# A state-space layer and a gated FFN: the norm's shift on ScalarE, twelve products with C on GpSimd, a new order of jobs

## The chip, the cores and the metric

One core of a Trainium2 chip runs one program. The metric is the device time of one execution in microseconds (us). TensorE multiplies and transposes, VectorE and ScalarE work on 128 partitions side by side, GpSimd (POOL in the profile) does elementwise products too, and SyncE (SP) issues the DMAs.

## What is computed

For 16 sequences of 1024 tokens with 256 channels: a selective scan with 16 states per channel, a residual and a layer norm, then a gated FFN with quantized weights, a residual and a second norm. The reference, cut:

```python
xz = jnp.einsum('btd,pd->btp', x, W_xproj)         # 64 for dt, 16 B, 16 C
dt = jax.nn.softplus(jnp.einsum('btr,dr->btd', dt_raw, W_dt) + b_dt)
dA = jnp.exp(dt[..., None] * A)
dBx = dt[..., None] * Bm[:, :, None, :] * x[..., None]
def step(h, inp):
    h = dA_t * h + dBx_t
    y = jnp.einsum('bds,bs->bd', h, C_t)
out = ys + Dp * x
x = _layernorm(x + out)
h = jax.nn.silu(gate) * up                          # 256 -> 768 -> 256
x = _layernorm(x + jnp.einsum('bsh,dh->bsd', h, wd))
```

A layer norm is (x - mean) * rstd, written in the kernel as x * rstd + shift with shift = -mean * rstd.

## The kernel before

Tokens come in 32 chunks of 512, two per sequence. An even chunk starts its scans from zero (`par` 0), the odd one from the last column of the even one's, which ScalarE keeps in `h_carry` (`carry`, L490). The Python loops write out all 32 chunks for each engine.

A chunk is 16 units, one for each state s. Channels lie on the partitions in two halves (q = 0, 1). For a state: ScalarE makes the decay exp(dt * a) (`decay`, L504); dt * x * B comes from GpSimd (`times_b`, L398, read from `b_bc`, rows of B that a DMA spreads over the partitions) or, for the six `K_STATES`, from ScalarE in token layout (`times_b`, L518) and TensorE, which transposes it into `p_da` (`ub_transposed`, L896). VectorE scans each half (L699, 1024 in all). The product with C is GpSimd's for the states of `POOL_STATES` (`times_c`, L408) and VectorE's for the other five (L707), with C spread by TensorE transposes into `p_c` (L905). TensorE sums all states in `p_y` (L922).

`p_da` has one PSUM bank for each half. A decay of a state that is not in `K_STATES` goes there too, and waits until the scan before has read the bank. Decays of `K_STATES` go to `da_k` in SBUF, `DA_LEAD` units ahead.

The other jobs belong to the chunk before (norm 1, gate, up, hidden), to the one two before (down, norm 2, store) or to the next one (transpose, projection, softplus, dt, u). `AT` gives each a unit and a zone in it (up to 5 zones, in each engine's own order); an engine's queue is in that order, and nothing overtakes. Their sequence: x is transposed, copied (`x_out`), projected; `rank_out` and `bc_out` copy out; `project_dt`, three activations and `dt_of` (VectorE, L675) give dt; `u_of` is GpSimd's (L387). Norm 1: `z_out`, statistics (L713) and means (L717) on VectorE, log and exp on ScalarE (L547, L552), `shifts` on VectorE for both norms in one operation of 8 columns, four normalizations (L529), transposes (`x1_transposed`), `x1_high` (ScalarE, L534), `x1_low` (VectorE, L727), six gate products (L953), each with a silu (L538) behind a table load, a table load back (`exp_table`, L542), six up products (L964) and six hidden products (L733). Gate and up share the two banks of `p_m`, so gate j waits for silu j-2. Then down (L977), `residual` (L740) and norm 2 (L559).

SyncE issues the spread of B in runs of states (L335) and of C by state (L342), each as soon as its buffer is free. A store waits in the same queue at unit `STORE_AT`. The shift, as it stands (L722):

```python
def shifts(call, k=slice(0, 2)):
    dve.wait_ge(s_rstd, call)
    nc.vector.scalar_tensor_tensor(shift[:, k, :], mean_var[:, k, :, 0], -1.0, rstd[:, k, :],
                                   ALU.mult, ALU.mult).then_inc(s_ln, 1)
```

## Time and profile before

| | |
|---|---|
| median of 3 runs | 1906.5 us (1903.86 to 1908.56) |
| profiled execution | 1904.62 us, span 1902.8 us |
| busy: PE, DVE, ACT, POOL | 1703.2 (90%), 1754.1 (92%), 1599.5 (84%), 1639.2 (86%) us |
| first scan to the end of the last | 27.0 to 1854.5 us |
| granted TensorE clock | 0.984 of full speed |

The names PE, DVE, ACT and POOL stand for TensorE, VectorE, ScalarE and GpSimd. In a row of a timeline the columns are the start in us, the time taken, engine, line, operation, what it writes and reads, how many are merged, and in brackets how long the engine stood idle before it and who ended that. In a row of a group the numbers behind the bars are busy us and mean ns of one, and the engine's idle us before them. Neighbours on one engine overlap by 0.05 to 0.1 us in the records, so the distance of two starts is the cost of the first.

### The profile page before, as it was taken

How to read it: one execution, taken by the hardware profiler on the slowest of the kernel's cores; microseconds unless marked ns; L12 is line 12 of the kernel's file. 1: busy time of each engine (PE TensorE's matmuls, PEld its weight loads, DVE VectorE, ACT ScalarE, POOL GpSimd, SP SyncE). 2: the span in 40 equal slices, each digit the busy share in tenths (PEclk: the TensorE clock that was granted, in tenths of full speed). 3: DMA queues.
4: the chain of work that ended last, by engine and by line, in shares of the span. 5: the costliest groups of instructions: out<-in, count | busy, mean ns of one | idle time of the engine just before them, and what ended most of it. 6: DMA issues, size and time to landing. Idle time of an engine off the chain costs nothing. (4 is left out here: it accounts for less than half of the span.)

```text
span 1902.8 us, 33164 instructions
## 1 busy us (share of the span) xinstructions
PE 1703.2 (90%) x11048; PEld 1339.9 (70%) x11048; DVE 1754.1 (92%) x2060; ACT 1599.5 (84%) x2992; POOL 1639.2 (86%) x710
## 2 busy tenths in 40 slices
PE   5789999998999999999998999989999999999977
PEld 3566777776777776777776777766777777777765
DVE  4999999999999999999999999999999999999993
...
GB/s 240 128 93 76 141 135 136 83 108 100 141 135 129 96 100 103 140 135 137 83 113 96 141 135 130 96 99 102 141 135 135 81 110 101 141 135 118 73 12 23
DMA packets 107419, 216.51 MB, mean 114 GB/s; under 512 B 10129, under 2 KB 44530, under 8 KB 107250
## 3 DMA queue, kind: packets, MB, share of 16 engines
...
q14 instruction: 79, 0.65, 0.1%
HBM read 195.48 MB, written 18.87 MB: 113 GB/s over the span
## 5 line engine op out<-in xcount | busy, mean ns | idle before, releaser
L408 POOL TENSOR_TENSOR h<-h,c_bc 128x1024 f32<-128x1024 f32 x352 | 830.3, 2368 | 122.3 <-ACT h_carry L490 62.3
L398 POOL TENSOR_TENSOR ub<-u,b_bc 128x1024 f32<-128x1024 f32 x320 | 753.3, 2368 | 0.1
L504 ACT ACTIVATE p_da<-dt,neg_a 128x512 f32<-128x512 f32 x640 | 435.1, 683 | 126.9 <-DVE h L699 121.2
L922 PE MATMUL p_y<-ident,h 128*128 128x128 f32 x4096 | 530.4, 278 | 5.2 <-POOL h L408 3.8
L922 PEld LDWEIGHTS p_y<-ident,h 128*128 128x128 f32 x4096 | 478.5, 144 | 37.6 <-issue 19.8
L699 DVE TENSOR_TENSOR_SCAN h<-p_da,h_carry,ub 128x512 f32<-128x512 f32 x320 | 392.6, 1264 | 6.6 <-ACT p_da L504 4.3
L699 DVE TENSOR_TENSOR_SCAN h<-p_da,ub 128x512 f32<-128x512 f32 x320 | 375.7, 1206 | 20.3 <-ACT p_da L504 13.0
L977 PE MATMUL p_o<-wt_down,hid 128*128 128x256 f32 x1536 | 347.3, 379 | 2.4 <-DVE res L740 1.6
L518 ACT ACTIVATE ub_t<-u_t,bc_t 128x256 f32<-128x256 f32 x768 | 341.6, 496 | 0.0
L977 PEld LDWEIGHTS p_o<-wt_down,hid 128*128 128x128 f32 x1536 | 286.8, 190 | 53.1 <-issue 14.7
L896 PE MATMUL p_da<-ident,ub_t 128*128 128x128 f32 x1536 | 236.2, 278 | 79.3 <-ACT ub_t L518 49.0
L504 ACT ACTIVATE da_k<-dt,neg_a 128x512 f32<-128x512 f32 x384 | 269.9, 711 | 0.0
L896 PEld LDWEIGHTS p_da<-ident,ub_t 128*128 128x128 f32 x1536 | 174.6, 142 | 129.7 <-ACT ub_t L518 81.2
L699 DVE TENSOR_TENSOR_SCAN h<-da_k,h_carry,p_da 128x512 f32<-128x512 f32 x192 | 237.2, 1263 | 2.7 <-PE p_da L896 2.1
L699 DVE TENSOR_TENSOR_SCAN h<-da_k,p_da 128x512 f32<-128x512 f32 x192 | 225.9, 1204 | 0.8 <-issue 0.3
L707 DVE TENSOR_TENSOR h<-h,p_c 128x1024 f32<-128x1024 f32 x160 | 190.8, 1192 | 0.7 <-ACT h_carry L490 0.6
L733 DVE SCALAR_TENSOR_TENSOR hid<-p_m,hid 128x512 f32<-128x512 f32 x188 | 125.2, 680 | 62.1 <-PE p_m L964 61.8
L964 PE MATMUL p_m<-x_t,wt_up 128*128 128x512 f16 x744 | 180.8, 379 | 0.1
L953 PE MATMUL p_m<-x_t,wt_gate 128*128 128x512 f16 x744 | 173.1, 378 | 0.3 <-ACT hid L538 0.3
L905 PE MATMUL p_c<-ident,bc_t 128*128 128x128 f32 x640 | 99.3, 279 | 72.2 <-DVE h L707 72.2
L387 POOL TENSOR_TENSOR u<-dt,x_t 128x1024 f32<-128x1024 f32 x32 | 75.7, 2365 | 91.2 <-DVE dt L675 91.2
L538 ACT ACTIVATE hid<-p_m 128x512 f32<-128x512 f32 x190 | 110.0, 597 | 49.4 <-PE p_m L953 48.9
...
## 6 DMA issues: line engine op xcount, KB each, us to landing
c_bc<-bc_rows_dram SPq DMA_DIRECT2D x352, 256.0 KB, 6.3
...
```

The source lines that it names most:

```text
L398: nc.gpsimd.tensor_tensor(ub[:, i % UB_SLOTS, :, :], u[:, par, :, :], b_bc[:, i:i + 1, :].broadcast_to([P, DH, T]), ALU.mult).then_inc(s_u ...
L408: nc.gpsimd.tensor_tensor(h[:, s % H_SLOTS, :, :], h[:, s % H_SLOTS, :, :], c_bc[:, i:i + 1, :].broadcast_to([P, DH, T]), ALU.mult).then_i ...
L504: nc.scalar.activation(da, dt[:, par, q, :], ACT.Exp, scale=neg_a[:, q, s:s + 1]).then_inc(done, 1)
L518: nc.scalar.activation(ub_t[:, i % K_SLOTS, k, :], u_t[:, k, :], ACT.Identity, scale=bc_t[:, par, k, s:s + 1]).then_inc(s_ubt, 1)
L699: nc.vector.tensor_tensor_scan(h[:, s % H_SLOTS, q, :], da, dbx, initial, ALU.mult, ALU.add).then_inc(s_scan, 1)
L707: nc.vector.tensor_tensor(h[:, s % H_SLOTS, :, :], h[:, s % H_SLOTS, :, :], p_c[:, :, :].broadcast_to([P, DH, T]), ALU.mult).then_inc(s_hc ...
L733: nc.vector.scalar_tensor_tensor(hid[:, j, :], p_m[:, j % 2, :] if bank is None else bank, 1.0 / (QUANT * X1_SCALE), hid[:, j, :], ALU.mul ...
L896: ins = nc.tensor.transpose(p_da[:, q, k * P:(k + 1) * P], ub_t[:, i % K_SLOTS, k, q * P:(q + 1) * P], ident[:, :])
L922: ins = nc.tensor.matmul(p_y_tok[:, k, q * P:(q + 1) * P], h[:, s % H_SLOTS, q, k * P:(k + 1) * P], ident[:, :], start=(s == SUM_ORDER[0] ...
L953: ins = nc.tensor.matmul(p_m[:, j % 2, :], wt_gate[:, n % DH, j * P:(j + 1) * P], x1_t[:, n // DH, n % DH, :], start=(n == 0), stop=(n == ...
L964: ins = nc.tensor.matmul(p_m[:, j % 2, :], wt_up[:, n % DH, j * P:(j + 1) * P], x1_t[:, n // DH, n % DH, :], start=(n == 0), stop=(n == 2 ...
L977: ins = nc.tensor.matmul(p_o[:, k % 2, :], hid[:, j, k * P:(k + 1) * P], wt_down[:, j, :], start=(j == 0), stop=(j == NH - 1))
```

## The change

- `shifts` is now 8 ScalarE activations of one column, -mean * rstd with the scale read from `rstd`. VectorE makes the negated means ahead of it (`negate`, one operation on 8 columns of one tensor).
- State 5's product with C goes from VectorE to GpSimd.
- `K_STATES` has 7 and 13 for 9 and 14. Slots are counted on over the chunks.
- `first_wait` issues a wait only where its engine has not yet waited for that value. In places waits change their order.
- `carry` is one unit later on ScalarE, behind the jobs of zone 0.
- Most entries of `AT` move.
- At the start VectorE makes `u` and the first product with B. At the end the last chunk's hidden values get a buffer of their own, the silus go ahead of norm 2 of the chunk before, TensorE's order is changed, and norm 2 and the store go in two halves.

The diff, cut (the many `first_wait` lines are of the form shown):

```diff
-POOL_STATES = (0, 1, 2, 3, 4, 7, 9, 10, 11, 13, 14)
+POOL_STATES = (0, 1, 2, 3, 4, 5, 7, 9, 10, 11, 13, 14)
 
 
 UB_AHEAD = 3
 
 C_LAG = 1
+CARRY_LAG = 1
+CARRY_ZONE = 0
...
-    "weights": (7, 1), "x_transposed": (0, 4), "x_out": (0, 2), "project": (2, 1), "rank_out": (4, 0),
-    "bc_out": (3, 1), "project_dt": (3, 3), "softplus_abs": (5, 1), "softplus_exp": (5, 1),
-    "softplus_log": (5, 3), "dt_of": (7, 0), "u_of": (7, 0), "u_transposed0": (12, 2), "u_out0": (14, 0),
-    "u_transposed1": (14, 3), "u_out1": (14, 2), "z_out": (2, 0), "stats1": (4, 0), "mean1": (5, 1),
-    "norm_log": (6, 0), "norm_exp": (6, 0), "shifts": (6, 1), "norm1_0": (6, 2), "norm1_1": (7, 1),
-    "norm1_2": (7, 1), "norm1_3": (7, 1), "x1_transposed": (8, 0), "x1_high": (8, 0), "x1_low": (8, 2),
-    "gate0": (9, 3), "gate1": (9, 3), "gate2": (10, 1), "gate3": (10, 2), "gate4": (10, 2), "gate5": (10, 2),
-    "silu0": (9, 1), "silu1": (9, 1), "silu2": (9, 2), "silu3": (10, 0), "silu4": (10, 0), "silu5": (10, 0),
-    "exp_table": (10, 0), "up0": (10, 2), "up1": (10, 2), "up2": (13, 0), "up3": (13, 1), "up4": (13, 4),
-    "up5": (14, 3), "hidden0": (11, 0), "hidden1": (11, 0), "hidden2": (13, 1), "hidden3": (14, 0),
-    "hidden4": (15, 0), "hidden5": (15, 0), "skip0": (8, 2), "skip1": (6, 1), "down0": (0, 3), "down1": (1, 0),
-    "down2": (1, 0), "down3": (1, 2), "down4": (2, 4), "down5": (2, 4), "down6": (3, 0), "down7": (3, 2),
-    "residual0": (1, 2), "residual1": (4, 2), "stats2": (5, 1), "mean2": (5, 2), "norm2_0": (11, 1),
-    "norm2_1": (11, 2), "norm2_2": (14, 3), "norm2_3": (15, 1), "bc_turned": (6, 0), "bc_cols": (9, 2),
+    "weights": (7, 1), "x_transposed": (0, 4), "x_out": (1, 3), "project": (2, 3), "rank_out": (3, 3),
+    "bc_out": (3, 0), "project_dt": (4, 0), "softplus_abs": (5, 1), "softplus_exp": (5, 1),
+    "softplus_log": (6, 1), "dt_of": (7, 2), "u_of": (8, 0), "u_transposed0": (12, 3), "u_out0": (14, 1),
+    "u_transposed1": (14, 3), "u_out1": (14, 1), "z_out": (2, 1), "stats1": (4, 1), "mean1": (5, 1),
+    "norm_log": (5, 2), "norm_exp": (6, 0), "negate": (6, 1), "shifts": (6, 1), "norm1_0": (7, 1),
+    "norm1_1": (7, 1), "norm1_2": (7, 1), "norm1_3": (7, 3), "x1_transposed": (8, 0), "x1_high": (8, 1),
+    "x1_low": (8, 2), "gate0": (9, 3), "gate1": (9, 3), "gate2": (10, 1), "gate3": (10, 1), "gate4": (10, 2),
+    "gate5": (10, 2), "silu0": (9, 0), "silu1": (9, 0), "silu2": (9, 1), "silu3": (9, 3), "silu4": (10, 0),
+    "silu5": (10, 1), "exp_table": (10, 1), "up0": (10, 2), "up1": (10, 2), "up2": (11, 1), "up3": (11, 3),
+    "up4": (13, 1), "up5": (13, 4), "hidden0": (11, 0), "hidden1": (11, 0), "hidden2": (12, 0),
+    "hidden3": (12, 2), "hidden4": (14, 2), "hidden5": (14, 2), "skip0": (8, 2), "skip1": (7, 2),
+    "down0": (0, 2), "down1": (0, 4), "down2": (1, 1), "down3": (1, 1), "down4": (3, 1), "down5": (3, 1),
+    "down6": (3, 2), "down7": (3, 2), "residual0": (2, 0), "residual1": (5, 0), "stats2": (5, 1),
+    "mean2": (5, 2), "norm2_0": (12, 0), "norm2_1": (12, 2), "norm2_2": (13, 0), "norm2_3": (14, 3),
+    "bc_turned": (5, 4), "bc_cols": (10, 3),
 }
...
-K_STATES = (2, 6, 9, 10, 14, 15)
+K_STATES = (2, 6, 7, 10, 13, 15)
 K_AHEAD = 2
 K_SLOTS = 2
-LATE = 13
-STORE_AT = 11
-DA_LEAD = {6: 2, 9: 3, 10: 2, 14: 2}
+LATE = 12
+STORE_AT = 7
+DA_LEAD = {6: 2, 7: 3, 10: 2}
...
-            if not isinstance(value, int) or value > 0:
+            if value > 0:
                 eng.wait_ge(s, value)
+
+        waited = {}
+
+        def first_wait(eng, s, value):
+
+            first = value > waited.get((eng, s.name), 0)
+            if first:
+                waited[eng, s.name] = value
+            return first
...
+        def slot_freed(eng, states, c, i, slots):
+
+            n = len(states) * c + i - slots
+            if n >= 0:
+                value = DH * units(n // len(states), states[n % len(states)])
+                if first_wait(eng, s_scan, value):
+                    eng.wait_ge(s_scan, value)
...
-                store(c)
+                for a in range(2):
+                    sp.wait_ge(s_out_ready, TT * (c + 1) + 2 * (a + 1))
+                    sp.dma_start(out_chunks[c][:, 2 * a:2 * a + 2, :],
+                                 res_n[:, 2 * a:2 * a + 2, :]).then_inc(s_out, 16)
             over_chunks(sp, step, tail)
-            sp.wait_ge(s_out, 16 * (CHUNKS + 1))
+            sp.wait_ge(s_out, 16 * (CHUNKS + 2))
...
             def times_c(c, s, par, batch):
                 i = POOL_STATES.index(s)
-                pool.wait_ge(s_c[i], 16 * (c + 1))
-                wait(pool, s_scan, 2 * units(c, s))
                 if par == 0:
                     pool.wait_ge(s_carry, units(batch, s))
+                elif first_wait(pool, s_scan, 2 * units(c, s)):
+                    pool.wait_ge(s_scan, 2 * units(c, s))
+                pool.wait_ge(s_c[i], 16 * (c + 1))
                 nc.gpsimd.tensor_tensor(h[:, s % H_SLOTS, :, :], h[:, s % H_SLOTS, :, :],
                                         c_bc[:, i:i + 1, :].broadcast_to([P, DH, T]),
                                         ALU.mult).then_inc(s_hc_pool, 1)
 
-            u_of(0, 0)
-            for s in range(UB_AHEAD):
+            for s in range(1, UB_AHEAD):
...
+            def shifts(call, norms=range(2), tiles=range(TT)):
+                act.wait_ge(s_rstd, call)
+                act.wait_ge(s_neg, call)
+                for n in norms:
+                    for t in tiles:
+                        ins = nc.scalar.activation(shift[:, n, t:t + 1], neg_mean[:, n, t:t + 1], ACT.Identity,
+                                                   scale=rstd[:, n, t:t + 1])
+                ins.then_inc(s_ln, 1)
+
+            def norm2(c, call, k, halves=2):
+                if first_wait(act, s_ln, call):
+                    act.wait_ge(s_ln, call)
+                if first_wait(act, s_res, 2 * c + halves):
+                    act.wait_ge(s_res, 2 * c + halves)
...
-                        if core and par == 0 and zone == 3:
-                            carry(c, s)
+                        if zone == CARRY_ZONE:
+                            cq, sq, pq = unit_at(c, s, -CARRY_LAG, par)
+                            if pq == 0 and (core if s >= CARRY_LAG else prev):
+                                carry(cq, sq)
 
             def tail(c):
                 z_out(c)
                 norm_log(c + 1, c + 1, 0, slice(0, 1))
                 norm_exp(c + 1, slice(0, 1))
+                shifts(c + 1, range(1))
                 for k in range(TT):
                     norm1(c, k, x_in)
                 x1_high(c)
+                for j in range(NH):
+                    silu(c, j, tail_ps[j % 4], tail_hid)
+                exp_table()
                 norm_log(c + 2, 0, c, slice(1, 2))
                 norm_exp(c + 2, slice(1, 2))
-                for j in range(NH):
-                    silu(c, j, tail_ps[j % 4])
+                shifts(c + 2, range(1, 2))
                 for k in range(TT):
                     norm2(c - 1, c + 2, k)
-                exp_table()
-                norm_log(c + 3, 0, c + 1, slice(1, 2))
-                norm_exp(c + 3, slice(1, 2))
-                for k in range(TT):
-                    norm2(c, c + 3, k)
+                for a in range(2):
+                    act.wait_ge(s_mean[1], c + 1 + a)
+                    half = slice(2 * a, 2 * a + 2)
+                    nc.scalar.activation(log_var[:, 1, half], mean_var[:, 1, half, 1], ACT.Ln,
+                                         bias=eps[:, :]).then_inc(s_log_var, 1)
+                    act.wait_ge(s_log_var, c + 3 + a)
+                    nc.scalar.activation(rstd[:, 1, half], log_var[:, 1, half], ACT.Exp,
+                                         scale=-0.5).then_inc(s_rstd, 1)
+                    shifts(c + 3 + a, range(1, 2), range(2 * a, 2 * a + 2))
+                    for k in range(2 * a, 2 * a + 2):
+                        norm2(c, c + 3 + a, k, a + 1)
...
                 i = DVE_STATES.index(s)
                 dve.wait_ge(s_c_ps, ND * c + (i + 1))
-                wait(dve, s_scan, 2 * units(c, s))
                 if par == 0:
                     dve.wait_ge(s_carry, units(batch, s))
+                elif first_wait(dve, s_scan, 2 * units(c, s)):
+                    dve.wait_ge(s_scan, 2 * units(c, s))
                 nc.vector.tensor_tensor(h[:, s % H_SLOTS, :, :], h[:, s % H_SLOTS, :, :],
                                         p_c[:, :, :].broadcast_to([P, DH, T]),
                                         ALU.mult).then_inc(s_hc_dve, 1)
...
-            def shifts(call, k=slice(0, 2)):
-                dve.wait_ge(s_rstd, call)
-                nc.vector.scalar_tensor_tensor(shift[:, k, :], mean_var[:, k, :, 0], -1.0, rstd[:, k, :],
-                                               ALU.mult, ALU.mult).then_inc(s_ln, 1)
+            def negate(call, c1, c2, k=slice(0, 2)):
+                wait(dve, s_mean[0], c1)
+                wait(dve, s_mean[1], c2)
+                wait(dve, s_ln, call - 1)
+                nc.vector.tensor_scalar_mul(neg_mean[:, k, :], mean_var[:, k, :, 0], -1.0).then_inc(s_neg, 1)
...
+            dve.wait_ge(s_dt, 1)
+            dve.wait_ge(s_xt, 1)
+            nc.vector.tensor_tensor(u[:, 0, :, :], dt[:, 0, :, :], x_t[:, 0, :, :], ALU.mult).then_inc(s_u, 1)
+            dve.wait_ge(s_u, 1)
+            dve.wait_ge(s_b[0], 16)
+            nc.vector.tensor_tensor(ub[:, 0, :, :], u[:, 0, :, :], b_bc[:, 0:1, :].broadcast_to([P, DH, T]),
+                                    ALU.mult).then_inc(s_ub_first, 1)
...
                 norm_mean(0)
+                negate(c + 1, c + 1, 0, slice(0, 1))
                 residual(c - 1, 0)
-                shifts(c + 1, slice(0, 1))
                 x1_low(c)
                 residual(c - 1, 1)
-                dve.wait_ge(s_res, 2 * c)
+                if first_wait(dve, s_res, 2 * c):
+                    dve.wait_ge(s_res, 2 * c)
                 norm_stats(1, res)
                 dve.wait_ge(s_stats[1], TT * c)
                 norm_mean(1)
-                shifts(c + 2, slice(1, 2))
+                negate(c + 2, 0, c, slice(1, 2))
                 for j in range(NH):
-                    hidden(c, j, tail_ps[(NH + j) % 4])
+                    hidden(c, j, tail_ps[(NH + j) % 4], tail_hid)
                 for a in range(2):
+                    half = range(2 * a, 2 * a + 2)
                     residual(c, a, x_in)
-                dve.wait_ge(s_res, 2 * (c + 1))
-                norm_stats(1, res)
-                dve.wait_ge(s_stats[1], TT * (c + 1))
-                norm_mean(1)
-                shifts(c + 3, slice(1, 2))
+                    dve.wait_ge(s_res, 2 * c + a + 1)
+                    norm_stats(1, res, half)
+                    dve.wait_ge(s_stats[1], TT * c + 2 * (a + 1))
+                    norm_mean(1, half)
+                    dve.wait_ge(s_mean[1], c + 1 + a)
+                    nc.vector.tensor_scalar_mul(neg_mean[:, 1, 2 * a:2 * a + 2], mean_var[:, 1, 2 * a:2 * a + 2, 0],
+                                                -1.0).then_inc(s_neg, 1)
...
-                for i in range(6):
+                for i in range(4):
                     down(c - 1, i // 2, i % 2, CHUNKS)
                 x1_transposed(c, False, True, x_in)
+                for i in range(4, 6):
+                    down(c - 1, i // 2, i % 2, CHUNKS)
+                for j in range(4):
+                    tail_gate(c, j)
                 for i in range(6, 8):
                     down(c - 1, i // 2, i % 2, CHUNKS)
-                for j in range(NH):
+                for j in range(4, NH):
                     tail_gate(c, j)
                 for j in range(NH):
                     tail_up(c, j)
                 for i in range(8):
-                    down(c, i // 2, i % 2, CHUNKS)
+                    down(c, i // 2, i % 2, CHUNKS, tail_hid)
```

## Rows read from the trace of the kernel before

**Rows 1.** busy time by stretch: an odd chunk, an even chunk.

```profile
993.30:1051.60 58.30, 52.35 (x347) 41.02 (x346) 55.99 (x65) 49.08 (x86) 51.93 (x23) 1.00 0.35 117
1051.60:1107.30 55.70, 51.48 (x344) 40.77 (x343) 52.77 (x65) 50.33 (x100) 50.41 (x23) 1.00 0.37 117
```

**Rows 2.** timeline of VectorE in the even chunk from 1051.63.

```profile
1051.63 2.31 DVE L699 TENSOR_TENSOR_SCAN h<-p_da,ub 128x512 f32<-128x512 f32 x2
...
1090.38 0.69 DVE L733 SCALAR_TENSOR_TENSOR hid<-p_m,hid 128x512 f32<-128x512 f32 x1 [1.85 <-PE p_m L964]
...
1092.15 5.88 DVE L699 TENSOR_TENSOR_SCAN h<-p_da,ub 128x512 f32<-128x512 f32 x5 [0.22 <-ACT p_da L504]
```

**Rows 3.** timeline of ScalarE in the same even chunk.

```profile
1063.68 0.58 ACT L461 COPY rank_t<-p_m 64x512 f32<-64x512 f32 x1
1064.17 0.91 ACT L518 ACTIVATE ub_t<-u_t,bc_t 128x256 f32<-128x256 f32 x2
...
1083.72 1.28 ACT L538 ACT_TABLE_LOAD   x1
```

**Rows 4.** timeline of ScalarE and VectorE in the odd chunk from 993.26.

```profile
1006.07 0.91 ACT L518 ACTIVATE ub_t<-u_t,bc_t 128x256 f32<-128x256 f32 x2
...
1027.05 1.28 ACT L538 ACT_TABLE_LOAD   x1
...
1036.11 5.98 DVE L699 TENSOR_TENSOR_SCAN h<-p_da,h_carry,ub 128x512 f32<-128x512 f32 x5 [0.22 <-ACT p_da L504]
```

**Rows 5.** waits of ScalarE from 1006.0 to 1027.1.

```profile
ACT p_da L504 <- DVE h L699: 1.3, 3, 0.7
ACT x L529 <- DVE shift L722: 0.6, 1, 0.6
```

**Rows 6.** timelines: the shift in four chunks, one GpSimd product.

```profile
98.25 5.08 DVE L722 SCALAR_TENSOR_TENSOR shift<-mean_var,rstd 128x8 f32<-128x8 f32 x1
100.92 2.38 POOL L408 TENSOR_TENSOR h<-h,c_bc 128x1024 f32<-128x1024 f32 x1
...
1014.30 2.08 DVE L722 SCALAR_TENSOR_TENSOR shift<-mean_var,rstd 128x8 f32<-128x8 f32 x1
...
1072.37 0.47 DVE L722 SCALAR_TENSOR_TENSOR shift<-mean_var,rstd 128x8 f32<-128x8 f32 x1 [0.30 <-ACT rstd L552]
...
1813.33 4.67 DVE L722 SCALAR_TENSOR_TENSOR shift<-mean_var,rstd 128x8 f32<-128x8 f32 x1
```

**Rows 7.** groups of instructions over the whole span.

```profile
L490 ACT COPY h_carry<-h 128x2 f32<-128x2 f32 x256 | 46.1, 180 | 0.7 <-DVE h L699 0.3
L717 DVE BATCH_NORM_AGGREGATE mean_var<-stats 128x2 f32<-128x6 f32 x256 | 23.0, 152 | 0.1
L547 ACT ACTIVATE log_var<-mean_var,eps 128x8 f32<-128x8 f32 (+1 forms) x34 | 9.9, 292 | 25.0 <-DVE mean_var L717 25.0
L552 ACT ACTIVATE rstd<-log_var 128x8 f32<-128x8 f32 (+1 forms) x34 | 7.1, 208 | 1.1
L1043 PE MATMUL p_m<-x_t,wt_gate 128*128 128x512 f16 x16 | 3.8, 378 | 1.8 <-ACT hid L538 1.8
```

**Rows 8.** the page, its parts 5 and 6.

```profile
L408 POOL TENSOR_TENSOR h<-h,c_bc 128x1024 f32<-128x1024 f32 x352 | 830.3, 2368 | 122.3 <-ACT h_carry L490 62.3
...
c_bc<-bc_rows_dram SPq DMA_DIRECT2D x352, 256.0 KB, 6.3
```

**Rows 9.** timeline of VectorE at the start: the first scan.

```profile
26.96 1.22 DVE L699 TENSOR_TENSOR_SCAN h<-p_da,ub 128x512 f32<-128x512 f32 x1 [4.96 <-POOL ub L398]
```

**Rows 10.** the chain that ended last, its end (start us, us, what).

```profile
1894.80 1.42 DVE stats L713 x4
...
1898.51 0.98 ACT res_n L559 x2
```

**Rows 11.** one line's instructions: the casts (ns min/median/max).

```profile
L671 DVE CAST hid<-hid x2: 952/956/959, 13.5 to 14.4; 128x1536 f32<-128x1536 int32 x2
L671 DVE CAST res<-res x1: 555/555/555, 15.2 to 15.2; 128x768 f32<-128x768 int32 x1
```

190 lines of the change are left out of this document (113 added, 77 removed).

## The prediction

> **What bounds the kernel now.** I read the busy time of each engine in two neighbouring chunks first. The time is made of 32 chunks of 512 tokens, and each chunk is 16 units, one for each state. Chunks come in pairs: an even one of 55.7 us and an odd one of 58.4 us, whose scans start from a carried state. VectorE is busy 52.8 us of the one and 56.0 of the other, GpSimd 50.4 and 51.9, TensorE 51.5 and 52.4, ScalarE 50.3 and 49.1 [rows 1]. So VectorE leads, but four engines lie within some 6 us, and an engine's total does not say which wait ends last. For that I follow one chunk along VectorE and ScalarE.
>
> In the even chunk from 1051.63 VectorE stands still in one place only: for `hidden0`, 1.85 us [rows 2]. Everything ahead of that wait is a chain. ScalarE has no idle time put down to any other engine between its first product with B of state 6, at 1064.17 (12.54 us into the chunk), and the table load ahead of the first silu, at 1083.72 (32.09) [rows 3]. The silus then pace the gate products, and a second table load and a decay stand between the last silu and the scan of state 11, at 1092.15 (40.52). From the first table load to that scan it is 8.43 us, of work that the change leaves as it is. After it VectorE works nearly without idle time for 15.2 us to the chunk's end. So **an even chunk is VectorE's for units 11 to 3, and ScalarE's for units 4 to 10.**
>
> In the odd chunk the same stretch on ScalarE goes from 1006.07 (12.8 us into the chunk) to 1027.05 (33.8), with 1.9 us of waiting for VectorE in it, 0.6 of that for the shift [rows 4, 5]. The scan of state 11 is at 1036.11, 42.85 into the chunk [rows 4]. This stretch was set by VectorE.
>
> **The shift.** It works on 8 elements, and takes 2.08 us in the odd chunk, 0.47 in the even one, 5.08 in chunk 1 and 4.67 in the last [rows 6]. In chunk 1 the last of GpSimd's products ended at 103.30, the shift at 103.33. So it waits for GpSimd, and there for more than two products in a row, each of 2.4 us. Both its inputs lie in SBUF.
>
> **The change, part by part.**
>
> Shift to ScalarE: VectorE loses 2.55 us a pair and gets a negation of 8 elements; one SBUF input, as in the aggregations of 0.15 us [rows 7]. I take 0.1, and the other case is a rival. ScalarE gets 8 activations of one column, each with a scale read from memory. No row has one. The nearest: the exp of 8 columns with a fixed scale lasts 208 ns, the log with a bias from memory 292, the carry's copy 180 [rows 7]. Back to back an operation overlaps the next by 0.09 us (the copy at 1063.68 lasts 0.58, the next starts 0.49 later [rows 3]). So one costs between 0.09 (a copy's spacing) and 0.2 us (292 less the overlap). I take 0.19, since the scale's read is like the log's bias: 1.5 us, with the wait of the first normalization for the last of them 1.6. They stand in unit 6, inside ScalarE's stretch, ahead of four normalizations, so in an even chunk all of it is on the path. The Trainium skill ("ScalarE: Activation LUTs", What ACT_TABLE_LOAD costs) gives 186 ns for an activation, 93 more for each pointer operand and an overlap of 93, which is an estimate of 0.19 too.
>
> `rank_out` from unit 4 to unit 3: it leaves the head of ScalarE's stretch, 0.49 us (1063.68 to 1064.17) [rows 3]. Other jobs of the stretch change places, not number: states 6, 7 and 10 take the way over TensorE where it was 6, 9 and 10, still three products and six pairs of decays. The silus begin in unit 9, as before behind the decays of state 10.
>
> Twelve products on GpSimd: VectorE loses one product, 1.11 us in spacing, in unit 6; GpSimd gets one of 2.37, spacing 2.32. GpSimd then has 23 operations, 53.4 us a chunk [rows 8]. TensorE loses four transposes, 0.6 us. VectorE's saving lies in the stretch that ScalarE sets: nothing in an even chunk, all of it in an odd one up to the point where ScalarE sets that too.
>
> Repeated waits dropped: two scans, each behind two to four waits, take 2.31 us together and leave no gap [rows 2], so I take nothing; bounds 0 and 0.3 us a chunk less.
>
> Jobs moved: `dt_of` goes behind the scans of unit 7. Walking the new order with the spacings of the rows, the x1 transposes start when `norm1_3` ends (27.0), `x1_high` at 28.5 and `x1_low` at 29.6, still ahead of the table load; I find no new wait there over 0.4 us. The two later hidden products come two units earlier, in time for their up products. The carries come one step later on ScalarE. In even chunks that of state 8 falls behind two silus, near 35.5, so VectorE's product of state 8 waits 2 us from 33.4; VectorE would stand before `hidden0`, near 40, anyway, so that is taken from idle time and costs 0 (2 if that wait were gone). GpSimd's products of states 9 and 10 wait for theirs too, in GpSimd's slack. On SyncE's queue the store goes ahead of the transfers of units 7 to 10. These are then issued near the end of a chunk, and are used from unit 5 of the next one, over 15 us later against landings of 6.3 us [rows 8]: nothing.
>
> **The sum for a middle chunk.** Even: ScalarE's stretch starts at 12.0, not 12.54, and its 19.55 us become 21.05 (1.6 more, 0.1 less as a carry moves behind the silus), so the table load is at 33.0, where it was 32.09: 0.9 us longer, 56.6. Odd: start 12.3, work 19.1 plus 1.6, no wait left, table load at 33.0 for 33.8; and the third gate product need not wait for a transpose of state 10 (0.65 us). Together 1.45 us shorter, 56.9. In both the scan of state 11 is then near 41.4. **The gain of the odd chunks is half eaten by the even ones:** 15 times +0.9 and 14 times -1.45 is -6.8; with 0.1 a chunk for small waits, about -9 us over chunks 2 to 30.
>
> **Ends.** Chunk 1: its shift of 5.08 goes, and other waits will take up a part, so -3 (bounds -1, -5). Last chunk: ScalarE has little to do there, and the 4.67 of the shift, the 1.11 of a product and a wait for `x1_high` go, -6 (bounds -3, -8). Start: `u` and the first product with B on GpSimd, for which the first scan waits 4.96 us [rows 9], become two VectorE operations of 1.2; ScalarE's transposed work and the second scan gain only 1.2 of the 2.4. With the product less in chunk 0: -2 (bounds -1, -4). Tail: x1 no longer waits behind the residual for its shift; the gate products lose the 1.8 us in which TensorE stood until the first silu [rows 7]; the last statistics go in halves, so of 4.7 us behind the last residual (1894.80 to 1899.49) 3.1 are left [rows 10]. Downs of the last chunk end 2.4 us earlier: -4 in all (bounds -2.5, -6).
>
> Sum: -9 - 3 - 6 - 2 - 4 = **-24 us**. The profiled execution took 1904.6 us (span 1902.8), which gives 1880.6; it stands 1.9 under the median of the three runs, so **1882**.
>
> **Rivals.**
> 1. *ScalarE's additions are cheap or its stretch has slack.* At 0.09 us each the shifts cost 0.7, the middle chunks gain 0.8 more each: 1882 - 24 = 1858. If VectorE sets the path throughout, the pair loses its 2.5 + 2.2 us in full (less 0.2), 4.5 for my 0.6: some 58 less, 1824 [rows 6, 7]. For: VectorE has the most busy time in rows 1. Against: rows 3.
> 2. *GpSimd becomes the bound.* 53.4 us of work in a chunk of 56.7 leaves 3.3 of idle time, and it waits 5.3 and more in a chunk now (rows 1: 55.7 less 50.4), for `dt_of` and for carries. If these waits stay, a chunk is some 57.4 on average over both kinds, 0.7 more: 1904. For: both waits are in the new order too. Against: with waits at fixed places a later GpSimd waits less.
> 3. *The negation meets the same lock as the shift.* The casts of the weights take 956 ns for 1536 columns and 555 for 768, 0.52 ns a column, half of what a scan or product needs: some one-input operations of VectorE in SBUF work at twice the rate [rows 11]. If the negation does, it waits in unit 6 until GpSimd's run of products (now three: state 4's with C, state 9's with B, state 5's with C) ends, as in chunk 1: from 20.4 to 25.4 into the chunk. VectorE then reaches `dt_of` 5 us late, `x1_high` comes at 31.3 for 28.5, the table load near 35.8 for 33.0. 2.8 us a chunk, 29 times, and 3 and 5 us in chunk 1 and the last: 1882 + 89 = **1971, slower**. It decides from about 2 us of waiting, which is the slack of `x1_low`. Against it: the aggregations, with one input in SBUF too and beside running products, are at 0.15 us in the mean of 256 [rows 7]. The Trainium skill ("SBUF — State Buffer", Who interferes with whom) says just this: tensor_scalar can run in a two-port mode and then shares an exclusive lock with GpSimd. By that rule the change would not do what it says. The trace shows the lock for two inputs and the double rate for a cast, neither for this form.
>
> **Chances.** Forecast 0.54; rival 1 0.18; rival 2 0.12; rival 3 0.16. The range 1842 to 1912 holds the forecast with the bounds of its terms, the cheap half of rival 1 and rival 2, and leaves out rival 3 and VectorE as bound. A measurement here tells 0.3% (6 us) from nothing. Faster 0.71, same 0.13 (rival 2 and the worst of the forecast's ends), slower 0.16.
>
> **What would show it.** The negation at 0.1 to 0.2 us, or at 2 to 5 ending with a GpSimd product. In the chunk's windows, even and odd both near 56.7. The idle time of VectorE before `hidden0` growing from 1.85 to some 3 us, and ScalarE without idle time in units 4 to 8. The shift activations spaced at 0.19 us. GpSimd's idle time shrinking to 3 us a chunk. The forecast fails if the scan of state 11 is not near 41.4 us into its chunk, by a ScalarE that is faster through unit 6 than its rows say, or by one that waits.

## The result: slower, by the rival that had 0.16

| | before | after |
|---|---|---|
| median of 20 runs, us | 1904.1 (1902.4 to 1908.6) | 1934.1 (1908.4 to 1939.8) |
| ratio, with its 95% interval | | 1.0134 [1.0115, 1.0154] |
| profiled execution, us (span) | 1904.6 (1902.8) | 1930.0 (1928.2) |
| granted clock, mean | 0.984 | 0.968 |

The time is outside my range of 1842 to 1912, and on the other side of "no change": slower by 1.3%, clear of the noise. The ratio leaves out the five runs after that are over 1.5% above the fastest of that kernel, so it is below the 1.016 of the two medians. The changed kernel also varies five times as much from run to run as the one before (31 us against 6).

Two rows of the groups of instructions by line (busy us, mean ns of one, idle time before), the first of after, the second of before, name the cause:

```profile
L795 DVE TENSOR_SCALAR neg_mean<-mean_var 128x8 f32<-128x8 f32 (+1 forms) x33 | 92.4, 2799 | 0.1
```

```profile
L722 DVE SCALAR_TENSOR_TENSOR shift<-mean_var,rstd 128x8 f32<-128x8 f32 (+1 forms) x34 | 46.5, 1369 | 5.7 <-ACT rstd L552 5.7
```

I had taken the negation of 8 elements at 0.1 us. Its mean is 2.8 us, twice that of the shift that it replaces. One odd chunk of after, as a timeline of all engines (start, us, engine, line, and in brackets the idle time ahead of it and what ended it), where [rows 6] has the shift at 2.08:

```profile
1142.69 2.36 POOL L442 TENSOR_TENSOR h<-h,c_bc 128x1024 f32<-128x1024 f32 x1
...
1143.79 5.88 DVE L795 TENSOR_SCALAR neg_mean<-mean_var 128x8 f32<-128x8 f32 x1
...
1145.01 2.34 POOL L431 TENSOR_TENSOR ub<-u,b_bc 128x1024 f32<-128x1024 f32 x1
...
1147.31 2.33 POOL L442 TENSOR_TENSOR h<-h,c_bc 128x1024 f32<-128x1024 f32 x1
1149.59 3.76 DVE L769 TENSOR_TENSOR_SCAN h<-da_k,h_carry,p_da 128x512 f32<-128x512 f32 x3
1149.77 1.59 ACT L602 ACTIVATE shift<-neg_mean,rstd 128x1 f32<-128x1 f32 x8 [4.61 <-DVE neg_mean L795]
...
1150.91 1.12 PE L987 MATMUL p_da<-ident,ub_t 128*128 128x128 f32 x4 [6.09 <-DVE h L769]
...
1154.54 2.37 POOL L421 TENSOR_TENSOR u<-dt,x_t 128x1024 f32<-128x1024 f32 x1 [4.89 <-DVE dt L742]
```

The negation starts 1.1 us into one GpSimd product, and lasts past the ends of two, until the third ends at 1149.64 and GpSimd has no next one. ScalarE meanwhile waits 4.61 us for it with the shifts, TensorE 6.09 for a scan behind it, and later GpSimd 4.89 for `dt_of`, which is late too: **all four engines stand, one after the other, for one operation of 8 elements.** The same row in chunk 1, in an even chunk and in the last:

```profile
98.12 7.46 DVE L795 TENSOR_SCALAR neg_mean<-mean_var 128x8 f32<-128x8 f32 x1
...
1087.82 0.51 DVE L795 TENSOR_SCALAR neg_mean<-mean_var 128x8 f32<-128x8 f32 x1
...
1840.81 8.40 DVE L795 TENSOR_SCALAR neg_mean<-mean_var 128x8 f32<-128x8 f32 x1
```

In all 15 even chunks from chunk 2 on it is 0.5 us, and in the 14 odd ones 5.9 us eleven times and 1.3 us three times; each time it ends within 0.1 us of the end of a product. Behind the last product, in the tail, the same form takes 0.17 us (this line: ns min/median/max, first and last start):

```profile
L896 DVE TENSOR_SCALAR neg_mean<-mean_var x2: 169/169/169, 1917.2 to 1923.4; 128x2 f32<-128x2 f32 x2
```

The busy times of the two kinds of chunk, in the columns of [rows 1] (us, then PE, PEld, DVE, ACT, POOL, then the granted clock):

```profile
1067.40:1122.80 55.40, 51.34 (x341) 40.30 (x339) 51.80 (x64) 50.96 (x108) 51.27 (x23) 1.00 0.40 123
1122.80:1183.80 61.00, 53.30 (x344) 41.89 (x343) 58.68 (x64) 49.99 (x94) 55.81 (x25) 0.94 0.38 117
```

VectorE's "busy" time in the odd chunk includes the wait, so 58.7 looks like work. In the even chunk, where the negation waits only 0.5 us, the new order takes 55.4 us for the 55.7 of [rows 1]. The clock in the odd one is 0.94 on average; in the 7 us from 1147.0, which begin inside the 6 us in which TensorE stands idle, it is 0.52, mostly the lower level of 1.2 GHz:

```profile
1147.00:1154.00 7.00, 3.09 (x16) 3.09 (x17) 6.96 (x5) 4.20 (x14) 2.65 (x2) 0.52 0.05 16
```

For all that follows I take the span apart at the first scan of each chunk (us; "even" and "odd" are means over chunks 2 to 30; every row comes from one profiled execution):

| kernel | first scan | chunk 0 | chunk 1 | even (15) | odd (14) | last | tail |
|---|---|---|---|---|---|---|---|
| before | 26.96 | 50.17 | 61.56 | 55.77 | 58.39 | 61.93 | 48.30 |
| after | 24.70 | 53.05 | 63.45 | 55.61 | 60.34 | 63.45 | 44.64 |
| e1, reduction | 24.59 | 55.65 | 56.08 | 55.84 | 55.66 | 54.59 | 44.65 |
| e3, GpSimd waits | 24.88 | 53.21 | 57.56 | 55.74 | 56.17 | 57.08 | 44.65 |
| e4, shifts doubled | 24.94 | 55.77 | 57.55 | 57.94 | 57.51 | 55.97 | 47.41 |
| e6, shift alone, reduction | 25.06 | 50.07 | 59.52 | 57.41 | 58.17 | 57.54 | 52.04 |
| e7, shift alone, multiplication | 25.59 | 50.22 | 62.75 | 57.87 | 59.97 | 62.05 | 50.37 |
| e8, e1 with 11 products | 22.88 | 55.18 | 56.09 | 55.43 | 56.14 | 55.30 | 44.65 |
| e9, shift on GpSimd | 24.76 | 55.75 | 55.43 | 54.27 | 55.01 | 54.29 | 44.65 |
| e10, after with 11 products | 24.80 | 56.08 | 60.86 | 55.43 | 60.18 | 63.65 | 44.65 |

### The profile page after: what moved, and what is told of

It is laid out like the page before. It is cut to its first block and busy times, and to the rows that moved or that the text cites. A ratio compares the mean times of both kernels' runs of the same rounds, so it can differ in the third digit from the quotient of the medians.

```text
span 1928.2 us, 30962 instructions
## 1 busy us (share of the span) xinstructions
PE 1704.6 (88%) x10920; PEld 1340.0 (69%) x10920; DVE 1768.7 (92%) x2031; ACT 1627.2 (84%) x3254; POOL 1710.9 (89%) x740
## 5 line engine op out<-in xcount | busy, mean ns | idle before, releaser
L442 POOL TENSOR_TENSOR h<-h,c_bc 128x1024 f32<-128x1024 f32 x384 | 905.1, 2365 | 86.8 <-ACT h_carry L528 59.8
L987 PE MATMUL p_da<-ident,ub_t 128*128 128x128 f32 x1536 | 243.6, 285 | 135.6 <-DVE h L769 123.5
L1076 PE MATMUL p_o<-wt_down,hid 128*128 128x256 f32 x1488 | 342.8, 380 | 0.0
L1076 PEld LDWEIGHTS p_o<-wt_down,hid 128*128 128x128 f32 x1488 | 275.5, 190 | 48.9 <-issue 14.7
L778 DVE TENSOR_TENSOR h<-h,p_c 128x1024 f32<-128x1024 f32 x128 | 153.8, 1202 | 30.7 <-ACT h_carry L528 30.6
L1051 PEld LDWEIGHTS p_m<-x_t,wt_gate 128*128 128x128 f16 x744 | 64.9, 98 | 100.6 <-ACT hid L581 38.9
L421 POOL TENSOR_TENSOR u<-dt,x_t 128x1024 f32<-128x1024 f32 x31 | 73.4, 2369 | 61.9 <-DVE dt L742 61.5
```

The lines of the kernel that those rows point to most:

```text
L442: nc.gpsimd.tensor_tensor(h[:, s % H_SLOTS, :, :], h[:, s % H_SLOTS, :, :], c_bc[:, i:i + 1, :].broadcast_to([P, DH, T]), ALU.mult).then_i ...
L778: nc.vector.tensor_tensor(h[:, s % H_SLOTS, :, :], h[:, s % H_SLOTS, :, :], p_c[:, :, :].broadcast_to([P, DH, T]), ALU.mult).then_inc(s_hc ...
L987: ins = nc.tensor.transpose(p_da[:, q, k * P:(k + 1) * P], ub_t[:, k_slot(c, i), k, q * P:(q + 1) * P], ident[:, :])
L1051: ins = nc.tensor.matmul(p_m[:, j % 2, :], wt_gate[:, n % DH, j * P:(j + 1) * P], x1_t[:, n // DH, n % DH, :], start=(n == 0), stop=(n == ...
L1076: ins = nc.tensor.matmul(p_o[:, k % 2, :], hid[:, j, k * P:(k + 1) * P], wt_down[:, j, :], start=(j == 0), stop=(j == NH - 1))
```

## Experiments

**e1: the same negation in another form** (here and, in the same way, in the tail). The theory: a multiplication by a constant needs the port to SBUF that GpSimd's products use, and waits until their run is broken. A reduction over one element gives the same 8 numbers without it.

```diff
-nc.vector.tensor_scalar_mul(neg_mean[:, k, :], mean_var[:, k, :, 0], -1.0)
+nc.vector.tensor_reduce(neg_mean[:, k, :], mean_var[:, k, :, 0:1], AxisListType.X, ALU.add, negate=True)
```

> The changed kernel, in which only the form of the negation differs: the mean is negated by a reduction over a dimension of one element (with its result negated) and not by a multiplication with a constant; the same 8 elements, the same place, the same engine, SBUF to SBUF. Theory A (the negation waits for GpSimd's run of products at their common port to SBUF, and the reduction doesn't use that port): the negation takes 0.1 to 0.2 us everywhere, all odd chunks are the 56.2 us that the three undisturbed ones of the changed kernel have, chunk 1 and the last lose 7 us each: 1928 - 11 x 5.3 - 14 - 2 = 1854, between 1848 and 1866. Rival B (8 elements are late for another reason: VectorE waits ahead of it for data, or the new order of the token jobs is itself slower): the long operation stays whatever its form, 1920 to 1940. Rival C (any operation of VectorE between SBUF and SBUF waits for GpSimd): as B. My recorded forecast for the case of a negation that costs nothing was 1882.

Measured: 1853.7 us, 0.9727 [0.9713, 0.9742] of before. The instructions of the negation, by line (ns min/median/max, first and last start):

```profile
L795 DVE TENSOR_REDUCE neg_mean<-mean_var x33: 133/135/157, 99.3 to 1829.0; 128x8 f32<-128x8 f32 x31, 128x4 f32<-128x4 f32 x2
```

One operation's form is the whole loss: 80 us between the medians of two kernels that differ in nothing else. In this form the negation never takes over 157 ns, beside the same products of GpSimd, so rivals B and C fall. The Trainium skill ("SBUF — State Buffer", Who interferes with whom) states that `tensor_scalar` can enter two-port modes and so contend for a pair of ports shared with GpSimd, and that `tensor_reduce` never does on this chip. Both halves agree with the rows: 5.88 us and 0.135.

**e3: GpSimd waits for the multiplication.** The form stays; only GpSimd's run is broken ahead of its product in unit 6.

```diff
+if s == 6 and (prev or last):
+    pool.wait_ge(s_neg, c)
 if core and (sa >= UB_AHEAD or nxt) and sa in B_STATES:
     times_b(ca, sa, pa)
```

> The changed kernel, the negation a multiplication as before, but GpSimd waits for the negation ahead of its product with B in unit 6. So the negation meets one running product at most. Theory A: it ends at the end of that product, 0.5 us in even chunks and 1.3 us in odd ones, GpSimd loses under 0.3 us a chunk; odd chunks near 56.2 and no other change: 1852 to 1868, within 0.4% of the kernel with the reduction. If the order or ScalarE's shifts were the cause instead, odd chunks stay near 61 and the time at 1920 to 1940.

Measured: 1861.0 us, 0.9766 [0.9751, 0.9780]. Timelines of GpSimd and VectorE in an odd chunk:

```profile
1106.41 2.35 POOL L442 TENSOR_TENSOR h<-h,c_bc 128x1024 f32<-128x1024 f32 x1
1108.88 2.35 POOL L431 TENSOR_TENSOR ub<-u,b_bc 128x1024 f32<-128x1024 f32 x1
...
1107.50 1.30 DVE L797 TENSOR_SCALAR neg_mean<-mean_var 128x8 f32<-128x8 f32 x1
```

As expected: the negation ends with the product, at 1108.80, and GpSimd goes on at 1108.88. It is 1.3 us in all 14 odd chunks. Adding a wait to GpSimd took 73 us off the kernel. In chunk 1 the negation comes earlier, passes one end of a product and stops where the added wait stands, at 4.16 us.

**e2: are the dropped waits to blame?** In the helper `first_wait`:

```diff
-return first
+return value > 0
```

> The changed kernel with every repeated wait put back (each engine waits again for what it has already waited for, the negation stays a multiplication). Theory A1 (a run of GpSimd products shuts the negation out whatever stands between them): as the changed kernel, 1920 to 1940, negation near 5.9 us in most odd chunks. Rival A2 (only products without a wait between them follow each other so closely that the negation doesn't get in; the dropped waits are what turned the short wait into a long one): the negation gets in at the next end of a product, 1.3 us in odd chunks, which are then near 56.2: 1860 to 1875.

Measured: 1940.0, 1.0188 [1.0153, 1.0223]. A1 holds: the long negations are there with all waits in place (5.9 us in 11 of the 14 odd chunks, 1.3 in three, and 8.8 in chunk 1).

**e5: and what are the waits worth?** The same edit on e1.

> The kernel with the reduction in place of the multiplication (1853.7), and every repeated wait put back. It prices the dropped waits. My prediction took them at nothing, with bounds 0 and 0.3 us a chunk: 1854 to 1863. The changed kernel with its multiplication gave 1934 and with the waits put back 1940, so the rival, 0.2 us a chunk, gives 1860, and the even and odd chunks of the trace are then each 0.2 longer than 55.8 and 55.7.

Measured: 1855.6, 0.9746 [0.9733, 0.9760], whose interval overlaps that of e1. By the trace a chunk is 0.1 (even, 55.92 for 55.84) and 0.2 us (odd, 55.89 for 55.66) longer, 4 us over the middle chunks, inside my bounds of 0 to 0.3 a chunk. The medians differ by only 2: in the traces, the stretch up to the end of chunk 0 is 3 us shorter with the waits, for no known reason. The 6 us between after and e2 say nothing here: the runs of the one scatter over 31 us and those of the other over 17.

**e4: are ScalarE's shifts on the path?** The 8 activations of e1, done twice.

```diff
+for n in norms:
+    for t in tiles:
+        nc.scalar.activation(shift_2[:, n, t:t + 1], neg_mean[:, n, t:t + 1], ACT.Identity, scale=rstd[:, n, t:t + 1])
 for n in norms:
     for t in tiles:
         ins = nc.scalar.activation(shift[:, n, t:t + 1], ...)
```

> The kernel with the reduction, in which ScalarE computes all 8 shifts twice (8 more activations of one column a chunk, into a tile that nobody reads). It prices the shifts on the path. By the steps of my prediction (units 4 to 10 are set by ScalarE in even and odd chunks, 0.19 us for one) each chunk grows by 1.5 us: 45 us over the kernel with the reduction, some 1900. If VectorE sets these units now, or ScalarE has slack there, it grows by less than 10 us in all. In between, the part of each kind of chunk can be read from its length.

Measured: 1918.4, 1.0065 [1.0048, 1.0081], 64.7 over e1. The timeline of ScalarE in one chunk:

```profile
1084.07 1.57 ACT L603 ACTIVATE shift<-neg_mean,rstd 128x1 f32<-128x1 f32 x8
1085.55 1.57 ACT L607 ACTIVATE shift<-neg_mean,rstd 128x1 f32<-128x1 f32 x8
```

Eight take 1.48 us from start to start, 0.185 each: my 0.19 holds. But a pair of chunks grew by 3.95 us, not 2.96. The rest comes with the clock: the two chunks around these rows have 0.97 each,

```profile
1061.60:1119.10 57.50, 52.48 (x341) 41.88 (x340) 51.59 (x64) 52.51 (x116) 51.28 (x23) 0.97 0.38 117
1119.10:1177.00 57.90, 53.28 (x344) 42.34 (x343) 53.23 (x64) 51.44 (x102) 55.82 (x25) 0.97 0.40 123
```

and in e1 there are even chunks of both kinds, from first scan to first scan 55.43 us at 1.00 and 56.11 at 0.97:

```profile
1028.40:1083.90 55.50, 51.29 (x342) 40.39 (x340) 51.54 (x65) 50.94 (x108) 51.45 (x23) 1.00 0.39 123
...
1139.50:1195.60 56.10, 52.53 (x341) 42.04 (x339) 51.46 (x64) 51.06 (x108) 51.39 (x23) 0.97 0.38 122
```

The two have the same instructions, so a fall of the clock costs 0.7 us there. Compared at an equal clock, the doubled shifts cost just their own length in both kinds: an even chunk at 0.97 takes 57.57 us for 56.11 in e1, an odd one at 1.00 takes 57.14 for 55.66. So all of the 1.48 is on the path. With doubled shifts TensorE waits for the normalized tile 96.7 us in all, with e1 50.6, and 21 of the 29 middle chunks have a clock below 1.00 instead of 9. A term that makes TensorE stand can thus cost more than its own length. It need not: in the kernel before, odd chunks at 0.97 and at 1.00 both take 58.4 us.

**e6 and e7: the shift's change alone.** The kernel before, with nothing changed but the shift: in e6 the negation is the reduction, in e7 the multiplication.

```diff
-dve.wait_ge(s_rstd, call)
-nc.vector.scalar_tensor_tensor(shift[:, k, :], mean_var[:, k, :, 0], -1.0, rstd[:, k, :], ALU.mult, ALU.mult)
...
+wait(dve, s_ln, call - 1)
+nc.vector.tensor_reduce(neg_mean[:, k, :], mean_var[:, k, :, 0:1], AxisListType.X, ALU.add, negate=True)
```

> The kernel before with the norm shift alone changed: VectorE negates the means by the reduction that doesn't wait for GpSimd, at the place of the old shift, and ScalarE computes the shift in 8 activations of one column. By the steps of my prediction: an even chunk gets ScalarE's 1.6 us on its path, 55.7 becomes 57.3; an odd one loses VectorE's 2.1 us up to the point where ScalarE sets it, whose work grows by 1.6 and of whose 1.9 us of waiting some 1.5 go: 58.4 becomes 58.5 (57.9 to 59); chunk 1 and the last lose 3 each. 1904 + 24 + 1 - 6 = 1923, so the shift's change alone is slower than before by some 1%. If ScalarE's additions are hidden (first rival): 1904 - 14 x 2 - 6 = 1870.

> As the run before it, but the negation is the multiplication of the changed kernel, which waits for GpSimd. In the kernel before, GpSimd has eleven products with C: at the place of the negation one product is running in odd chunks and GpSimd is idle behind it (0.5 us to the next product's start in even ones). Theory A, the length of the wait is the rest of GpSimd's unbroken run: 2.1 us in odd chunks and 0.5 in even ones, as the old shift; the time is that of the kernel with the reduction plus up to 2 us an odd chunk, and nowhere near the 5.9 us waits of the changed kernel. So the long waits need the twelfth product as well, behind which GpSimd's run at this place is three products. Rival: the multiplication waits longer than the old two-input shift wherever it stands; then 5 us and more also here, and a time above 1960.

e6: 1919.8, 1.0076 [1.0063, 1.0090]. Expected 1923; even chunks 57.4 for my 57.3, odd 58.2 for 58.5. The total fits partly by luck: the tail is 3.7 us longer and the start 1.9 shorter, and I had neither. **Even with a free negation, moving the shift to ScalarE alone makes this kernel slower**: it gives ScalarE 1.5 us where ScalarE sets the pace, for 2.1 us of VectorE in every second chunk, of which 0.2 are left.

e7: 1960.9, 1.0291 [1.0277, 1.0305]. The negation lasts 2.07 us in odd chunks and 0.86 in even ones, as A has it (0.5 expected for the latter; it comes earlier), so the rival, which had 5 us and more, falls by these lengths. The time is where the rival had put it, since the price was higher than "up to 2 us an odd chunk": +1.8 in odd chunks, +0.46 in even ones, and 3.2 and 4.5 in chunk 1 and the last: 40 us, 41 by the medians. The old shift was waited for by nobody for long (0.6 us, [rows 5]). The negation is: ScalarE's 8 shifts wait for it, with all of ScalarE's queue behind them.

```profile
1101.90 0.86 DVE L740 TENSOR_SCALAR neg_mean<-mean_var 128x8 f32<-128x8 f32 x1
...
1102.86 1.59 ACT L561 ACTIVATE shift<-neg_mean,rstd 128x1 f32<-128x1 f32 x8 [0.60 <-DVE neg_mean L740]
```

**e8 and e10: the twelfth product.** `5` is taken out of `POOL_STATES`, in e1 and in the changed kernel.

> The kernel with the reduction (1853.7), and the product with C of state 5 back on VectorE, in unit 6: eleven products on GpSimd. It prices the twelfth product where the negation costs nothing. By the steps of my prediction the product's 1.1 us lies in units that ScalarE sets, in both kinds of chunk once the shift is gone: nothing in an even chunk, 0 to 0.5 in an odd one, 1854 to 1861, and the same with what the last chunk's 1.1 us adds. The rival (VectorE sets these units): 1.1 us a chunk, 1888. A second rival (GpSimd sets them, the twelfth product costs): 1835.

> The changed kernel with its multiplication (1934), and the product with C of state 5 back on VectorE. Theory A: what shuts the negation out is GpSimd's unbroken run at that place, and the twelfth product is its last member. With eleven, the run ends one product earlier: the negation ends at 1.3 or 3.6 us in odd chunks and never at 5.9, in chunk 1 at 5.1 or less. The time is between that of this kernel with the reduction and 2.3 us a chunk over it: 1856 to 1900. Rival: how long it waits has to do with something else (the dropped waits, the state of the queue), the 5.9 us stay, 1930 to 1950.

e8: 1854.1, 0.9741 [0.9726, 0.9755], the same as e1. Odd chunks are 0.5 longer, even ones 0.4 shorter: they have no fall of the clock here, and take the same 55.43 us as those of e1 without one. In all, the twelfth product was worth nothing.

e10: 1923.0, 1.0099 [1.0080, 1.0118]. The negation is 3.6 us in 12 of the 14 odd chunks and 1.3 in two, never 5.9 (6.1 in the last chunk). An odd chunk:

```profile
1143.71 2.38 POOL L431 TENSOR_TENSOR ub<-u,b_bc 128x1024 f32<-128x1024 f32 x1
1146.04 2.37 POOL L442 TENSOR_TENSOR h<-h,c_bc 128x1024 f32<-128x1024 f32 x1
1148.37 2.34 POOL L431 TENSOR_TENSOR ub<-u,b_bc 128x1024 f32<-128x1024 f32 x1
...
1147.14 3.60 DVE L795 TENSOR_SCALAR neg_mean<-mean_var 128x8 f32<-128x8 f32 x1
```

One product less in the run, one product less of waiting: a negation that doesn't get in earlier waits for the rest of the run. But the time is above my 1856 to 1900, since these odd chunks are 60.6 us, 4.5 over the 56.1 of e8 for 3.5 of waiting. I had priced the wait at two thirds of its length. Most of these odd chunks have a clock of 0.97, those of e8 1.00.

**e11 and e12: the late carry.** In e1, VectorE's product of state 8 waits 2 us for its carry in each even chunk, as predicted. In these the carries go back to their old place, in e1 and in e9 (below).

```diff
-CARRY_LAG = 1
-CARRY_ZONE = 0
+CARRY_LAG = 0
+CARRY_ZONE = 3
```

> The kernel with the reduction (1853.7), with the carries back at their old place on ScalarE, at the end of each unit, so that the carry of state 8 stands ahead of the first silu again. VectorE's wait of 2 us for it in each even chunk (30 us in all) goes. By my prediction it was taken from idle time ahead of the first hidden product: VectorE waits there for TensorE instead, the chunk keeps its length, 1851 to 1859 (the carry's own 0.1 us now delays the silus). Rival: the wait was on the path, 15 times up to 2 us: 1825 to 1835.

> The kernel with the shift on GpSimd (1819.0) with the same return of the carries. There VectorE waits 1.5 us for the carry of state 8, 22.8 us in all. As above by my theory: no gain, 1816 to 1824. Rival: up to 22 us less, 1798 to 1805.

Measured: 1850.9, 0.9724 [0.9709, 0.9738], and 1819.2, 0.9555 [0.9540, 0.9571]: the same times as without the edit. VectorE's waits (total, times, longest), in e1, and then in e11, where the one for the carry is gone:

```profile
DVE hid L805 <- PE p_m L1063: 52.1, 62, 2.4
...
DVE h L778 <- ACT h_carry L528: 30.7, 16, 2.2
```

```profile
DVE hid L805 <- PE p_m L1063: 80.4, 62, 2.6
```

30.7 us of one wait went, and 28.3 came back as another: the wait was taken from idle time, as my step said. The 2.8 us that e11 is under e1 are within their intervals.

**e9: the shift off both engines.** If ScalarE sets units 4 to 10, its 8 activations are the next thing to take away. GpSimd can do them in one operation. This is e1 with the lines below on GpSimd, and without ScalarE's call of `shifts` in the chunks; the tail keeps its calls.

```diff
+if s == 6 and (prev or last):
+    pool.wait_ge(s_rstd, c)
+    pool.wait_ge(s_neg, c)
+    nc.gpsimd.tensor_tensor(shift[:, :, :], neg_mean[:, :, :], rstd[:, :, :], ALU.mult).then_inc(s_ln, 1)
```

> The kernel with the reduction (1853.7), in which GpSimd multiplies the 8 negated means by the 8 reciprocal deviations in one operation, ahead of its product with B in unit 6, and ScalarE's 8 activations go from the 31 middle calls. GpSimd waits there for the deviations, up to 1 us. If ScalarE sets units 4 to 10, as my prediction has it and as doubling the activations showed (+2.0 us a chunk), a chunk loses about 1.5 us: 1853.7 - 30 x 1.5 = 1809; the table load comes near 31.0 us into an even chunk instead of 32.5. If GpSimd (23 operations and one more, 54 us a chunk, and waits at fixed places) then sets the pace, the gain stops at chunks of about 55: 1830. If the gain is nothing, the doubling measured something else (the clock).

Measured: **1819.0, 0.9547 [0.9533, 0.9560]**, 4.5% faster than before and, with e12, the best of all kernels here. I had expected 1809, and 1830 if GpSimd then set the pace. GpSimd in an even chunk:

```profile
1031.89 0.20 POOL L461 TENSOR_TENSOR shift<-neg_mean,rstd 128x8 f32<-128x8 f32 x1 [0.73 <-ACT rstd L600]
1032.06 2.38 POOL L431 TENSOR_TENSOR ub<-u,b_bc 128x1024 f32<-128x1024 f32 x1
```

An even chunk loses 1.57 us against e1, 1.16 of it where e1's clock didn't fall, and an odd one 0.65, so less than the 1.48 of the activations: other work sets the pace behind that point. The table load is 31.35 us into the even chunk (1041.59 less 1010.24) for 32.51. The clock stays at the upper level from chunk 2 to the last, 1.00 in both kinds:

```profile
955.20:1010.20 55.00, 52.16 (x344) 40.54 (x343) 52.82 (x64) 48.51 (x86) 55.00 (x26) 1.00 0.42 128
1010.20:1064.50 54.30, 51.35 (x342) 40.32 (x341) 51.28 (x64) 49.63 (x100) 52.30 (x24) 1.00 0.40 126
```

**e13: which engine sets the pace then?** e9 with eleven products.

> The kernel with the shift on GpSimd (1819.0), and the product with C of state 5 back on VectorE. In that kernel GpSimd is busy 107.3 us of a pair of chunks of 109.3, VectorE 104.1. If GpSimd sets the pace there, the product on VectorE shortens a pair by up to 2 us, until VectorE with 106.3 us of work and its waits for the up products is the bound: 1805 to 1817. If units 4 to 10 are still ScalarE's and the rest VectorE's, nothing changes (1816 to 1822) or VectorE's 1.1 us a chunk come on top in the stretch from the shift to the scan of state 11: up to 1850. The product has been worth nothing where ScalarE had the shifts (1854.1 to 1853.7).

Measured: 1846.1, 0.9695 [0.9678, 0.9712]. GpSimd was busy 55.0 us of an odd chunk of 55.0 in e9, and still, moving a product from it to VectorE costs 27 us (even chunks 54.94, odd 56.14): VectorE has little room for the product's 1.1 us there (an even chunk grows by 0.7 and an odd one by 1.1). So the twelfth product is worth 27 us once ScalarE's shifts are gone, and nothing while they are there.

That GpSimd is no bound in e9 doesn't follow, since the product went to an engine that has little room for it. These are the engines' parts in the chain of work that ended last, as shares of the whole span, first of e1, where the chain reaches back to the start, then of e9, where it reaches back to 1521:

```profile
ACT 51%; PE 33%; DVE 8%; issue 7%; DMA 0%; DVEq 0%; ACTq 0%; SPq 0%
```

```profile
POOL 4%; ACT 4%; PE 4%; issue 2%; DVE 2%; ACTq 0%; DVEq 0%; POOLq 0%
```

GpSimd is not in the chain of e1, and in e9 it has the largest share, 62 us of it in chunks 28 and 29. In e12, with the same time, it has 9 us of the chain behind 1630. So in e9 several engines lie close together, and no run here gives GpSimd less work without giving VectorE more.

## Why the prediction failed

**The negation (0.1 us, "the other case is a rival").** This is the step that failed, and rival 3 names the mechanism. I chose by the nearest row, and took the wrong one as nearest: the aggregations [rows 7], because they too have one input in SBUF. What mattered was the form, and for it the casts at double rate [rows 11] were the neighbour. I had both rows, and gave the rival 0.16 because neither is of this form. Its cost if true was 89 us, so it should have carried more of the range.

**Rival 3's own price (1971).** Too high by 37, and 28 of these are its base: it stood on my 1882, where the kernel with a cheap negation takes 1854. The price itself, 89, is near the 80 measured, and this is luck. I had 81 for the 29 middle chunks, which cost 62 more than in e1, and 8 for chunk 1 and the last, which cost 16. In even chunks the negation gets in at the first end of a product and costs nothing (55.61 against 55.84 with the reduction). In odd ones it is 5.9 us, eleven times, and costs all of that (61.5 on average against 55.7, a part of it by the clock of 0.94): I sent its delay through VectorE alone, past `dt_of` and `x1_low`, whose slack of 2 us I subtracted. In fact ScalarE waits for it directly, with every decay and product with B of its queue behind the shifts, so there was no slack of 2 us to subtract: even the three short ones, 1.3 us, cost 0.5 us a chunk (56.15 for 55.66).

**The rest of the change, with the negation out of the way (e1), against the sum.**

| step | forecast | e1 |
|---|---|---|
| start, to the first scan | -2 | -2.4 |
| chunk 0 | 0 | +5.5 |
| chunk 1 | -3 | -5.5 |
| 15 even chunks | +13.5 | +1.1 |
| 14 odd chunks | -20.3 | -38.2 |
| last chunk | -6 | -7.3 |
| tail | -4 | -3.7 |
| all (forecast with 2 for small waits) | -24 | -50.5 |

That e1, 1854, is near the 1858 of rival 1's cheap half is luck as well: its reason was activations of 0.09 us, and they take 0.185.

- *ScalarE sets units 4 to 10, and 8 activations cost 1.5 us there*: right (e4), and the middle chunks of e6 came out as its steps say. Without the activations a chunk gives back 1.2 and 0.65 us (e9), so their last 0.3 to 0.8 us lie close to another bound.
- *The new order costs or gains nothing by itself*: wrong by about 1 us a chunk, the gain in both kinds. In even chunks the table load is at 32.5 for my 33.0, and from it to the scan of state 11 are 8.25 us at full clock, for 8.43. From that scan to the chunk's end it is 14.7 us, where I carried over 15.2. VectorE has the same work there, but before (first fence) it stands 0.22 us ahead of a scan, and 0.09 ahead of another; in e1 (second fence) both gaps are gone, and with them the overlap that each gap breaks. In odd chunks the table load is at 32.1 for 33.0. Which of the moved jobs did it was not taken apart.

```profile
1097.95 0.67 DVE L733 SCALAR_TENSOR_TENSOR hid<-p_m,hid 128x512 f32<-128x512 f32 x1
1098.83 1.22 DVE L699 TENSOR_TENSOR_SCAN h<-p_da,ub 128x512 f32<-128x512 f32 x1 [0.22 <-ACT p_da L504]
```

```profile
1074.25 0.67 DVE L805 SCALAR_TENSOR_TENSOR hid<-p_m,hid 128x512 f32<-128x512 f32 x1
1074.83 2.32 DVE L769 TENSOR_TENSOR_SCAN h<-da_k,p_da 128x512 f32<-128x512 f32 x2
```

- *Chunk 0*: I counted only the product less. In e1 VectorE stands 4.52 us for TensorE ahead of the scans of state 13, which takes the way over TensorE now; in after it stands 2.19 there. Chunk 0 is 2.9 us longer in after, 5.5 in e1, though the two kernels are alike up to there: this difference was not explained.

```profile
71.99 2.33 DVE L769 TENSOR_TENSOR_SCAN h<-da_k,p_da 128x512 f32<-128x512 f32 x2 [4.52 <-PE p_da L988]
```

- *Waits dropped*: 0.1 to 0.2 us a chunk (e5). I took them at nothing in one place and at 0.1 a chunk in the sum, which has -9 where -6.8 and 29 times 0.1 make -9.7. *The carry at no cost*: right (e11). *GpSimd bound (rival 2)*: not in e1 (e8, and GpSimd is not in its chain); open in e9 (e13).
- *Twelfth product*: nothing in even chunks, 0.5 in odd ones (e8); right.
- *The clock* had no term in my sum. It adds the 0.7 us of e1's slower even chunks, and a part of what each long negation costs: in after, odd chunks with 5.9 us take 5.3 more than those with 1.3, for 4.6 of waiting.

**What stays open.** Why a waiting negation gets in at the end of one product and not at another. All 15 even chunks let it in at the first end, half a microsecond after it started to wait; chunk 1, with the same half microsecond, not in three ends. In odd chunks it got in at the first end in 3 of 14, in e2 also in 3, in e10 in 2. This is likely why the changed kernel's time scatters over 31 us, where four runs of e1 lie within 3; it is not shown, since only one run of each kernel was traced. It isn't the dropped waits (e2), and where GpSimd had a wait that was not met yet, the negation always got in (e3). What decides otherwise was not found.
